# The B loads of a DLRM cross network, issued by ScalarE on its own DMA queue

## The reference

```python
e = stack([tbl_f[ids[:, f]] for f in range(24)], axis=1)      # X0: 1024 x 24 x 16
# three layers, H = 64 each; Xk starts as X0
Xk = einsum('bfd,bhd,fho->bod', X0, Xk, Wr); outs.append(Xk.sum(axis=2))
h = concat([z, dense_ctx], axis=1)                            # 1024 x (192 + 16)
h = relu(h @ W_top1 + b_top1)                                 # 512
h = relu(h @ W_top2 + b_top2)                                 # 256
y = h @ W_top3                                                # 1024 x 1
```

## Time and profile before

| | |
|---|---|
| median of three runs | 423.25 us (416.54 to 425.3) |
| the profiled execution | 421.92 us, of which its span 420.1 us |
| PE busy | 342.1 us (81%) |
| DVE busy | 288.5 us (69%) |
| ACT busy | 189.7 us (45%) |
| POOL busy | 233.2 us (55%), ends with the last gather near 300 us |
| moved by DMA | 73.63 MB, mean 175 GB/s |
| share of the DMA engines by SP's queue (q1) | 74.2% |
| share by POOL's queue (q0) | 3.2% |
| mean granted TensorE clock | 0.955 |
| B loads | 90 DMAs of 256 KB, 23.6 MB |

### The profile page before, as it was taken

How to read it: one execution, slowest core, us unless ns; L and a number is a source line. 1 busy time by engine, 2 the same in 40 slices (tenths; PEclk the granted TensorE clock), 3 DMA queues, 4 the chain that set the end, 5 groups by cost and what they waited for, 6 DMA issues and landing times.

```text
span 420.1 us, 6106 instructions
## 1 busy us (share of the span) xinstructions
PE 342.1 (81%) x2296; PEld 150.5 (36%) x2296; DVE 288.5 (69%) x277; ACT 189.7 (45%) x346; POOL 233.2 (55%) x252
## 2 busy tenths in 40 slices
PE   0045899438396969599999997999999999999997
PEld 0043422102041323244333433543444344443466
DVE  2001499129385959578987998798899999898700
ACT  1000026113335345273737573757556475745374
POOL 5775888888888888788788887677400000000000
PEclk9998899859886999999999999999999999999999
DMA  3355936499799998999799979998999799731000
GB/s 101 74 111 116 231 83 157 83 231 234 164 242 233 252 257 152 228 231 213 163 228 223 232 137 222 233 235 163 225 251 266 156 251 258 214 107 44 2 2 2
DMA packets 59263, 73.63 MB, mean 175 GB/s; under 512 B 31489, under 2 KB 36609, under 8 KB 59234
## 3 DMA queue, kind: packets, MB, share of 16 engines
q1 hardware_dynamic: 53090, 71.66, 74.2%
q0 software_dynamic: 6144, 1.59, 3.2%
HBM read 48.05 MB, written 1.58 MB: 118 GB/s over the span
## 4 chain that ended last, share of the span: by engine, by line
PE 68%; DMA 10%; issue 9%; POOL 3%; another core or an unknown queue 2%; ACT 2%; SPq 2%; DVE 1%; DVEq 0%; ACTq 0%
PE ps_x L370 44%; PE ps_tower L370 9%; PE ps_turn L370 6%; PE ps_b L370 5%; POOL x_rows L191 3%; DMA A<-x_scratch 3%; DMA B_sb<-x_sb 2%; DMA x_scratch<-x_rows 2%; PE ps_turn L415 2%; PE ps_turn L423 1%; SPq L256 1%; DMA C<-x_scratch 1%; DVE Z L337 1%; PE ps_tower L376 1%
## 5 line engine op out<-in xcount | busy, mean ns | idle before, releaser
L347 DVE TENSOR_TENSOR Z<-A,ps_b 128x1024 f32<-128x1024 f32 x192 | 222.0, 1214 | 29.5 <-remote 18.8
L191 POOL DMA_INDIRECT x_rows<-tbl,ids_sb x192 | 190.8, 994 | 62.6 <-issue 43.6
L370 PE MATMUL ps_x<-Z,w_sb 128*64 128x512 f32 x768 | 188.4, 609 | 1.7 <-issue 1.0
L337 DVE TENSOR_TENSOR Z<-A,C 128x1024 f32<-128x1024 f32 x48 | 58.1, 1224 | 75.5 <-DMA C<-x_scratch 37.4
L370 PEld LDWEIGHTS ps_x<-Z,w_sb 128*64 128x64 f32 x768 | 50.3, 139 | 84.3 <-issue 65.8
L370 PE MATMUL ps_x<-Z,w0s_sb 128*64 128x512 f32 x192 | 48.3, 626 | 24.4 <-DVE Z L337 23.9
L635 ACT ACTIVATE x_diag<-ps_turn,mask_sb 128x192 f32<-128x192 f32 x128 | 50.6, 606 | 9.9 <-PE ps_turn L423 9.8
L618 ACT COPY ps_b<-B_sb 128x1024 f32<-128x1024 f32 x45 | 46.4, 1030 | 9.8 <-DMA B_sb<-x_sb 5.9
L648 ACT COPY G<-ps_turn 128x416 f32<-128x416 f32 x31 | 15.7, 506 | 73.5 <-remote 45.8
L599 ACT COPY x_sb<-ps_x 128x512 f32<-128x512 f32 x16 | 9.4, 586 | 78.2 <-PE ps_x L370 78.2
L204 POOL MEMSET pause_sb<- 128x768 f32 x56 | 42.3, 756 | 3.6 <-DMA x_scratch<-x_rows 3.6
(11 more groups left out here) (48 smaller groups left out, 147.2 us busy)
## 6 DMA issues: line engine op xcount, KB each, us to landing
A<-x_scratch SPq DMA_DIRECT2D x48, 512.0 KB
B_sb<-x_sb SPq DMA_DIRECT2D x90, 256.0 KB
C<-x_scratch SPq DMA_DIRECT2D x32, 512.0 KB
x_rows<-tbl,ids_sb POOLq DMA_INDIRECT x192
x_quarters<-x_scratch SPq DMA_DIRECT2D x16, 96.0 KB
x_scratch<-x_rows SPq DMA_DIRECT2D x7, 192.0 KB
w_sb<-w SPq DMA_DIRECT2D x2, 384.0 KB
C<-x_scratch SPq DMA_DIRECT2D x2, 256.0 KB
```

The lines of the kernel that those rows point to most:

```text
L191: pool.indirect_dma_start(out=x0_rows[t % 2][:, f * D:(f + 1) * D], out_offset=None, in_=tables[f], in_offset=bass.IndirectOffsetOnAxis(ap ...
L337: nc.vector.tensor_tensor(Z[s % ZR][:, :], A[u % AS][i][:, :], C[u % 2][i][:, :], ALU.mult).then_inc(z_ready, 1)
L347: nc.vector.tensor_tensor(Z[s % ZR][:, :], A[u % AS][i][:, :], ps_b[j % 2][:, :], ALU.mult)\
L370: return nc.tensor.matmul(out, lhsT, rhs, start=start, stop=stop)
```

## The change

`load_b` moves from SP's list to ACT's. The DMAs, their source and destination, and their semaphore are the same; they now go out on ACT's queue. In SP's list the three places that called it are gone. In ACT's list, for slots u from 2 to 14, load_b(u + 1, 0) stands right after copy_x1(u + 1), load_b(u + 1, 1) right after copy_b(u, 1), and load_b(u + 1, 2) right after copy_b(u, 2), so that each follows the copy that frees its buffer; in slots 0 and 1 all three stand after copy_x1(u + 1). The wait for x1_copied now stands ahead of each k, and the wait for b_copied is one of ACT for its own earlier instruction.

```diff
--- before.py
+++ after.py
@@ -244,18 +244,6 @@
                 src = rows_of(0, FR * i, FR).rearrange("t f c -> (t f) c").unsqueeze(1)
                 sp.dma_start(half, src.to_broadcast([FR, FR, COLS])).then_inc(c2_in, 16)
 
-            def load_b(u, k):
-
-                j = k + 1
-                if k == 0:
-                    sp.wait_ge(x1_copied, u + 1)
-                if u > 1:
-                    sp.wait_ge(b_copied, (NJ - 1) * (u - 2) + k + 1)
-                for q in range(2):
-                    src = x1_sb[u % 2][H * q + j:H * (q + 1):NJ, :].unsqueeze(1)
-                    sp.dma_start(B_sb[k][:, HALF * q:HALF * (q + 1)], src.to_broadcast([HR, FR, HALF]))\
-                        .then_inc(b_in[k], 16)
-
             def load_quarters(u):
                 src = rows_of(u, 0, F).rearrange("t f (h c) -> (t f) h c", h=QUARTERS)
                 sp.dma_start(x0_quarters[u % 2][0:QUARTERS * F, :], src).then_inc(quarters_in[u % 2], 16)
@@ -280,8 +268,6 @@
             for u in range(2, UNITS):
 
                 if u == 2:
-                    for k in range(NJ - 1):
-                        load_b(u - 1, k)
                     store_tile(1)
                 if u % 2 == 0:
                     wait_stored(sp, u // 2)
@@ -292,9 +278,6 @@
                     if u >= AS:
                         sp.wait_ge(z_ready, made_x2(u - AS, NP2 - NI + i))
                     load_a(u, i)
-                if u > 2:
-                    for k in range(NJ - 1):
-                        load_b(u - 1, k)
                 if u % 2 == 1 and u + 1 < UNITS:
                     store_tile((u + 1) // 2)
                 sp.wait_ge(x0_turned, u - 1)
@@ -304,8 +287,6 @@
                                      (wt2_sb[:, :, :], wt2), (wt3_sb[:, :], wt3), (bt1_sb[:, :], bt1),
                                      (bt2_sb[:, :], bt2), (dense_sb[:, :], dense_t)):
                         sp.dma_start(dst, src).then_inc(tower_in, 16)
-            for k in range(NJ - 1):
-                load_b(UNITS - 1, k)
             sp.wait_ge(y_ready, GROUPS)
             sp.dma_start(out, y_sb[:, :]).then_inc(y_stored, 16)
             sp.wait_ge(y_stored, 16)
@@ -608,6 +589,17 @@
                 nc.scalar.copy(c[NI - 1][0:64, :], c[1][64:128, :]).then_inc(c_copied, 1)
                 nc.scalar.copy(c[NI - 1][64:128, :], c[0][0:64, :]).then_inc(c_copied, 1)
 
+            def load_b(u, k):
+
+                j = k + 1
+                act.wait_ge(x1_copied, u + 1)
+                if u > 1:
+                    act.wait_ge(b_copied, (NJ - 1) * (u - 2) + k + 1)
+                for q in range(2):
+                    src = x1_sb[u % 2][H * q + j:H * (q + 1):NJ, :].unsqueeze(1)
+                    nc.scalar.dma_start(B_sb[k][:, HALF * q:HALF * (q + 1)], src.to_broadcast([HR, FR, HALF]))\
+                        .then_inc(b_in[k], 16)
+
             def copy_b(u, k):
 
                 act.wait_ge(b_in[k], 32 * u)
@@ -729,11 +721,15 @@
                 towers = g > 0
                 if u > 0:
                     copy_x2(u - 1)
-                if 2 <= u < UNITS - 1:
+                first = 2 <= u < UNITS - 1
+                if first:
                     copy_x1(u + 1)
+                    load_b(u + 1, 0)
                 if u > 0:
                     copy_x2_rows(u - 1)
                     copy_b(u, 1)
+                if first:
+                    load_b(u + 1, 1)
                 if towers and w == 1:
                     relu_h1(g - 1, 0)
                 if towers and w == 2:
@@ -743,11 +739,15 @@
                 if u > 0:
                     copy_g(u - 1, 0)
                     copy_b(u, 2)
+                    if first:
+                        load_b(u + 1, 2)
                     copy_g(u - 1, 1)
                 if u == 1:
                     copy_c(2)
                 if u < 2:
                     copy_x1(u + 1)
+                    for k in range(NJ - 1):
+                        load_b(u + 1, k)
                 elif u + 2 < UNITS:
                     copy_c(u + 2)
                 if towers and w == 0:
```

## The result

The changed kernel took 426.14 us (median of four runs, 424.7 to 426.48), the kernel before 421.06 us with one run more (416.54 to 425.3). The ratio is 1.0196, 95% interval 1.0133 to 1.0258: slower, by more or less than 2% isn't settled. A ratio compares only runs within 1.5% of the fastest of their kernel, here two of the four of the kernel before (416.54 and 418.86 us); by the medians of all runs it is 1.012. The profiled execution took 424.7 us, its span 422.8, against 421.92 and 420.1 before: 2.7 us more.

A forecast was written before the change was run, and what follows sets the result against it. It took transfers to bound the kernel up to some 160 us and PE's matmuls from about 190 us. 421.92 + 0 + 0 + 2.5 = 424.4 us profiled, 425.8 as a median, stated as 425; range 417 to 436.

The forecast's parts named there:

- Issues taken from SP: In SP's list, 6 issues per unit, 3.6 us, go away; worth nothing, since SP waits for turn_x0 anyway.
- Issues on ACT at 0.6 us: In each ACT slot, six added issues take 3.6 us; at 0.6 us each they cost nothing.
- the cover: In ACT's tightest slot, u = 12, 0.4 us to spare for four issues before sum_g needs the copies.
- Rival 2: In ACT's slots from u = 2, issues cost more, 1.0 us each; about 10 to 15 us, 433; chance 0.12.
- B(2) beside A(3): Around 98 us, B(2) on ACT's queue no longer stands behind A(3); DVE gains 0 to 4 us here.
- sharing: Around 98 us, queues share the DMA engines; half of 247 GB/s brings B(2, 0)'s 0.52 MB in 4.2 us.
- The reading of the gather: At 110.06 us, a tile 2 gather beside SP's queued B(2) was storable 2.9 us later: a second queue escapes the backlog.
- B(3) before A(4): Around 120 us, B(3)'s bytes go ahead of or beside A(4), delaying cross1(4) on DVE and PE; +2.5 us, other end +0.3.
- PE carries the delay to the end: After cross1(4), A(5) and C(5) have several us to spare, so PE keeps the +2.5 us to the end.
- Rival 3: After SP's stores, ACT's issues are held up, 0.6 to 4.4 us for each of four tiles; 2 to 18 us; chance 0.12.

The follow-up runs named there:

- e1: The changed kernel with the B loads of units 1 to 3 back on SP; 428.9 us, ratio 1.0005 to the kernel before.
- g3: Kernel with 23 of 24 gathers of tiles 3 to 7 left out, B loads of units 4 to 15 on ACT, others on SP; 405.2 us.
- g1: The kernel before with 23 of 24 gathers of tiles 3 to 7 and their pauses left out; 406.41 us.
- e5: The changed kernel with each B load in four DMAs of half the bytes, so twice the issues; 452.54 us, ratio 1.0552.
- r1: The changed kernel measured a second time, unaltered, against the kernel before; 430.01 us, ratio 1.0048.
- e2: The kernel before with only the three B loads of unit 3 issued by ACT; 429.65 us, ratio 0.9973.
- g2: The changed kernel with 23 of 24 gathers of tiles 3 to 7 and their pauses left out; 406.3 us.
- g4: The kernel before with 23 of 24 gathers of tiles 3 to 7 left out and only unit 3's B loads on ACT; 406.79 us.
- e3: The kernel before with only the B loads of units 1 and 2 issued by ACT; 429.18 us, ratio 0.9931.
- e4: The changed kernel with the eight tower weight loads issued after A(4) instead of before C(4); 429.6 us, ratio 1.0102.
- h1: The kernel before with 23 of 24 gathers of tiles 3 to 7 replaced by POOL memsets; 407.06 us, ratio 0.9577.
- h2: The kernel before with all gathers but without POOL's pause memsets from tile 3 on; 442.0 us, ratio 1.0334.

## Why the prediction was right, and where not

The time, 426.14 us, lies near the 425 that was said, and the profiled execution came out at +2.7 us against +2.5. Much of that agreement is luck, as the steps show: e1's profile comes out at +3.0 us without the wait that was to cost the 2.5, and on the second measurement the change is worth +0.1% by the medians. The sum itself gave 425.8 as a median; the 0.8 us down to 425 have no reason in the working.

*Issues taken from SP, worth nothing.* Right as far as these runs can tell: e1 has twelve units' issues off SP and a ratio of 1.0005. Only the profiles without the gathers hint at a gain, 1.9 us (g3 against g1).

*Issues on ACT at 0.6 us, hidden.* Right: 622 ns by the median. From x1(12) at 334.24 to x1(13) at 353.48 a late slot takes 19.24 us, exactly as before (331.87 to 351.11). That the cover is about as thin as worked out is what e5 shows: doubling the issues costs 22.5 us, 1.7 for each of 13 slots, where four more issues of 0.62 us less the cover of 0.4 would make 2.1. Rival 2 is the case of e5, and did not come in.

*B(2) beside A(3), a gain of 0 to 4 us.* The gain was nothing, the lower end: the last product of cross1(3) starts at 112.61, in r1 at 111.77, against 112.06. B(2, 0) was ready at 109.37, not before 104.7 as sharing would have it. By the prediction's estimate half of 247 GB/s brings its 0.52 MB in 4.2 us, and it took 9.8 from its issue. That fits a B(2) that stood behind C(3) and A(3), which SP had issued by 87.87. The reading of the gather that landed 2.9 us after its issue, that a second queue shares at once, did not carry over to B loads on ACT's queue.

*B(3) before A(4), +2.5 us.* The mechanism is right and shown by e1 and e2: it comes with B(3) on ACT and goes without it. Its size was off. The start of the last product of cross1(4) moved by 9.5 us in the profile (146.14 against 136.6), where 4.3 was said (140.9). A missing term is SP's own issuing: with B(3) in the other queue the weights took 7.9 us (6.1 in e2) instead of 3.9, so C(4) and A(4) were issued later. I had held C(4) to its old time. In the first profile a late store (+3 us) came on top, which varies by itself: in r1, the same kernel, it left at 112.85. Where the store was on time that product started at 143.03 (r1), 143.46 (e2), 141.11 (g2) and 140.94 (g4), 0 to 2.6 us later than was said.

*"PE carries the delay to the end."* This is the step that failed. The loss of 8.75 us at x1(4) was 3.1 us one slot later, and e2 has the wait and no loss in its time. Without the gathers, g2 and g4 lose 4.8 us at x1(4) and are level with g1 by x1(10). Up to there PE does not set the pace alone, as I took it to from A(5) on. The step fails in part only: g2 against g3 has 1.8 of the 4.8 us left at x1(8), and PE does carry those, since they are 1.8 at x1(10) and 2.6 in the span. With the gathers the unknown waits cover all this; why they were 23.1 us instead of 45.8 on ACT in this one profile isn't shown. In r1 they were back at 43.9 us.

*Rival 3, ACT held up behind SP's store.* It fell. While SP's issue of the quarters stood for 3.05 us behind the store (116.44 to 119.49), ACT issued two loads in 1.27 us (116.52), and none of its 90 issues took over 1.62 us (1.89 in r1), where over 2 would have decided. That SP's slow issue waits for the store's small pieces, as the prediction has it, isn't shown.

What stays open: whether the change costs anything at all beyond noise. The first measurement says 1.3 to 2.6% (1.2% by the medians), the second 0 to 1% (0.1% by the medians). With the gathers nearly gone it costs nothing (406.3 against 406.41), and no part of it alone, e1 to e3, was slower than before. Whether e4's 1% is real is not known either. No version is shown to beat both kernels: g3's 402.4 us of span points to a gain of under 1% that these runs can't show.

## What to carry to other kernels

A second issuing engine changes the order of transfers: look for the load that was issued first because it was needed first. A wait that appears in the trace is a loss only if what comes after it had no slack; follow the distance between both kernels from one landmark to the next before you add it to the sum, and first see how far two profiles of one kernel lie apart at these landmarks. And issues that fit into a compute engine's gaps cost nothing that could be measured here, but 22 us when doubled.

## What was not expected of the hardware

What waits for PE's small matmuls is held up while POOL issues gathers. In the kernel before, the copy behind sum_g, 0.9 us of matmuls, waited for an unknown releaser a dozen times and started up to 5.9 us after the recorded matmuls (129.95 against 124.00), all before 300 us, where the gathers end; the waits go with the gathers (g1, 45.8 to 6.1 us) and not with POOL's memsets (h1), and 115 gathers fewer (77 instead of 192) are worth 23 us. Spaced by pauses they do less harm than in an unbroken chain, in which the copy behind one sum_g came 22 us late (h2). By what path a gather does this isn't shown.

The other surprise is that SP's own issues get slower once B(3) is issued by ACT (7.9 us for eight loads instead of 3.9). That B(3)'s place does it is shown by e1 and e2; the mechanism isn't. It need not be the second queue: in the kernel before, with all loads in SP's queue, the quarters issued soon after B loads and a store took 3.90 and 4.87 us (at 284.20 and 323.53) instead of 0.8, so that many bytes are under way may be enough. No run issued B(3) ahead of the weights from SP, which would tell.
